# Grouped-query attention scores on four row groups of TensorE, with the maximum and the subtraction merged

## The reference, cut to what matters

```
Q = (x @ Wq.T).reshape(B, S, HKV, G, HEAD_DIM)     # HKV = 4, G = 4
K = (x @ Wk.T).reshape(B, S, HKV, HEAD_DIM)
V = (x @ Wv.T).reshape(B, S, HKV, HEAD_DIM)
scores = einsum('bskgd,bswkd->bskgw', Q, K_win) * scale
attn = softmax(scores, axis=-1)
out = einsum('bskgw,bswkd->bskgd', attn, V_win).reshape(B, S, HQ * HEAD_DIM)
return out @ Wo.T
```

## Time and profile before

| | us |
|---|---|
| median of 3 runs | 1850.55 (1847.84 to 1853.06) |
| profiled execution, device time | 1847.98 |
| its span | 1846.2 |
| PE busy | 1664.0 (90%) |
| DVE busy | 809.1 (44%) |
| ACT busy | 492.9 (27%) |
| POOL busy | 407.7 (22%) |

### The profile page before, as it was taken

How to read it: one execution, slowest core, us unless ns; L and a number is a source line. 1 busy time by engine, 2 the same in 40 slices (tenths; PEclk the granted TensorE clock), 3 DMA queues, 4 the chain that set the end, 5 groups by cost and what they waited for, 6 DMA issues and landing times.

```text
span 1846.2 us, 22813 instructions
## 1 busy us (share of the span) xinstructions
PE 1664.0 (90%) x8086; PEld 1167.7 (63%) x8086; DVE 809.1 (44%) x1724; ACT 492.9 (27%) x953; POOL 407.7 (22%) x421
## 2 busy tenths in 40 slices
PE   5876899986799999999938999999899989998999
PEld 4532355555699999999934556766764446666444
DVE  3532787776311111111157650122365556675455
ACT  1234554441112221212114322223110035544000
POOL 0363876661211111211110000000010012232000
PEclk9989899996699999999968989999789999998999
DMA  5233565554234544313130000010000010000000
GB/s 168 68 93 102 138 153 124 139 128 142 83 138 160 189 160 160 140 50 137 41 106 1 0 29 0 1 46 1 1 1 1 1 46 1 1 1 1 12 18 20
DMA packets 59046, 129.17 MB, mean 70 GB/s; under 512 B 10563, under 2 KB 39268, under 8 KB 52388
## 3 DMA queue, kind: packets, MB, share of 16 engines
q1 hardware_dynamic: 54996, 116.96, 20.3%
q0 software_dynamic: 3936, 10.75, 1.8%
HBM read 196.35 MB, written 9.97 MB: 112 GB/s over the span
## 4 chain that ended last, share of the span: by engine, by line
PE 79%; DVE 10%; POOL 3%; SPq 2%; issue 2%; DMA 2%; ACT 2%; DVEq 0%; ACTq 0%; POOLq 0%
PE psum L686 41%; PE psum L972 13%; PE psum L718 8%; PE psum L781 5%; PE psum L902 2%; PE psum L696 2%; PE psum L897 2%; DVE work L1794 1%; DVE work L1650 1%; SPq L592 1%; DVE work L1793 1%; ACT work L1072 1%; PE psum L957 1%; POOL xn L1863 1%; PE psum L981 1%
## 5 line engine op out<-in xcount | busy, mean ns | idle before, releaser
L686 PE MATMUL psum<-work 128*128 128x128 f32 (+4 forms) x3528 | 481.5, 298 | 15.9 <-DMA work<-in_xp 15.9
L686 PEld LDWEIGHTS psum<-work 128*128 128x128 f32 (+1 forms) x3528 | 451.2, 192 | 34.0 <-DMA work<-in_xp 15.9
L972 PE MATMUL psum<-w_late,xn 128*128 128x512 f32 x544 | 241.4, 602 | 0.0
L1717 DVE TENSOR_TENSOR work<-sq,psum 128x512 f32<-128x512 f32 x82 | 56.4, 688 | 388.8 <-PE psum L686 388.8
L972 PEld LDWEIGHTS psum<-w_late,xn 128*128 128x128 f32 x544 | 103.2, 192 | 128.3 <-issue 118.8
L1650 DVE TENSOR_TENSOR_SCAN work<-psum,work 128x414 f32<-128x414 f32 (+1 forms) x160 | 160.4, 1060 | 47.6 <-POOL work L1885 24.0
L1885 POOL TENSOR_TENSOR work<-work 128x408 f32<-128x408 f32 (+1 forms) x160 | 161.7, 1038 | 64.9 <-PE psum L781 47.1
L1844 POOL TENSOR_TENSOR rs<-rs,power 128x4 f32<-128x4 f32 (+3 forms) x40 | 45.1, 1130 | 577.7 <-DVE rs L1344 548.0
L1534 DVE SCALAR_TENSOR_TENSOR h<-psum,gate,h 128x256 f32<-128x256 f32 x272 | 119.3, 480 | 106.3 <-PE psum L972 103.4
L1072 ACT ACTIVATE work<-psum 68x364 f32<-68x364 f32 (+10 forms) x266 | 113.2, 466 | 144.5 <-PE psum L686 66.9
L781 PE MATMUL psum<-work,xn 128*128 128x408 f32 (+1 forms) x320 | 136.6, 560 | 14.1 <-POOL work L1885 14.0
(11 more groups left out here) (255 smaller groups left out, 1961.5 us busy)
## 6 DMA issues: line engine op xcount, KB each, us to landing
work<-in_W SPq DMA_DIRECT2D x123, 1024.0 KB
work<-c_rows SPq DMA_DIRECT2D x48, 204.0 KB, 4.1
w_attn<-in_B SPq DMA_DIRECT2D x64, 128.0 KB, 2.5
w_attn<-in_A SPq DMA_DIRECT2D x64, 128.0 KB, 2.8
work<-c_rows SPq DMA_DIRECT2D x32, 238.0 KB, 4.0
w_attn<-in_A SPq DMA_DIRECT2D x64, 64.0 KB, 2.2
w_attn<-in_B SPq DMA_DIRECT2D x64, 64.0 KB, 2.8
work<-y_rows SPq DMA_DIRECT2D x8, 512.0 KB, 7.6
```

Source lines behind the costliest of these rows:

```text
L686: mm = pe.matmul(dst, lhs(k), rhs(k), start=(k == 0), stop=(k == parts - 1))
L972: mm = pe.matmul(dst.rearrange("p (e n) -> p e n", e=2), xn[:, k, i * P:(i + 1) * P], w_last[:, 2 * q:2 * q + 2, k, :], start=(k == 0), st ...
L1717: dve.tensor_tensor(hm[:, j % 2, 4 * q:4 * q + 4, :].rearrange("p k n -> p (k n)"), sa[:, i % 2], A.at(("e3", j, q)), ALU.mult).then_inc(s ...
```

## The change

The keys are kept as they come, in `k3` (68 columns per batch), with one copy per chunk and no memset. Scores of one batch are 12 matmuls: for each piece and head g, the 32 rows of that head on row group g of the array (`tile_position=(g * HPAD, 0)`), 68 columns, into bank g of a new ring S4 of four banks, so a bank holds one head's three pieces. All four banks belong to one batch. shift3 then is one maximum and one subtraction over 91 x 816. Ring T (banks 4, 5, 6) takes projections, transposes and out3, ring O (bank 7) the values' product, and the layer norm of L3F has banks 4 and 5. ACT does exp3(b+2) in iteration b, where it did exp3(b+3). DVE's order is sum3(b+1), shift3(b+3), add_h.

```diff
-        kblk = carve(KR * KV_HEADS * SEQ).rearrange("p (b g s) -> p b g s", g=KV_HEADS, s=SEQ)
+        k3 = carve(KR * SEQ).rearrange("p (b s) -> p b s", s=SEQ)
...
+        S4 = Banks(psum, [0, 1, 2, 3], tenants)
+        T = Banks(psum, [4, 5, 6], tenants)
+        O = Banks(psum, [7], tenants)
...
-        ln_ring = {L0A: F, L3A: W8}
+        ln_ring = {L0A: F, L3A: W8, L3F: Banks(psum, [4, 5], tenants)}
...
         def plan_s3(b):
-            for i in range(PIECES):
-                A.plan(("s3", b, i), (sem("s3_shifted"), PIECES * b + i + 1))
+            for g in range(KV_HEADS):
+                S4.plan(("s3", b, g), (sem("s3_shifted"), b + 1))
             step("s3", b)
...
-                plan_h("out3", L3A, c)
+                plan_h("out3", L3A, c, T)
                 plan_ln_after(L3F, c, 2)
             if b < BATCH:
-                B.plan(("o3", b), (sem("o3_kept"), b + 1))
+                O.plan(("o3", b), (sem("o3_kept"), b + 1))
...
+                banks = [S4.wait_free(pe, ("s3", b, g)) for g in range(KV_HEADS)]
                 for i in range(PIECES):
-                    dst = A.wait_free(pe, ("s3", b, i))
-                    pe.matmul(dst[0:PROWS, 0:KV_HEADS * SEQ],
-                              q3[:, c % 2, b - CHUNK_B0[c], PIECE0[i]:PIECE0[i] + PROWS], kblk[:, at3(b)],
-                              start=True, stop=True).then_inc(sem("s3_done"), 1)
+                    for g in range(KV_HEADS):
+                        rows = slice(g * HPAD, (g + 1) * HPAD)
+                        mm = pe.matmul(banks[g][0:PROWS, i * SEQ:(i + 1) * SEQ],
+                                       q3[rows, c % 2, b - CHUNK_B0[c], PIECE0[i]:PIECE0[i] + PROWS], k3[rows, at3(b), :],
+                                       start=True, stop=True, tile_position=(g * HPAD, 0))
+                mm.then_inc(sem("s3_done"), 1)
...
-            act.wait_ge(sem("pool_setup"), 6)
...
-                src = A.at(("k3", c))
-                for g in range(KV_HEADS):
-                    rows = slice(g * HPAD, (g + 1) * HPAD)
-                    ins = act.activation(kblk[rows, at3(CHUNK_B0[c]):at3(CHUNK_B0[c]) + CHUNK_BATCHES[c], g, :],
-                                         seqs(src[rows, 0:ntok(c)]), ACT.Copy)
-                ins.then_inc(sem("k3_kept"), 1)
+                copy(k3[:, at3(CHUNK_B0[c]):at3(CHUNK_B0[c]) + CHUNK_BATCHES[c], :], seqs(T.at(("k3", c))[:, 0:ntok(c)]), "k3_kept")
...
-            for b in range(AHEAD):
+            for b in range(AHEAD - 1):
                 exp3(b)
...
-                if b + AHEAD < BATCH:
-                    exp3(b + AHEAD)
+                if b + AHEAD - 1 < BATCH:
+                    exp3(b + AHEAD - 1)
...
             def shift3(b):
-                for i in range(PIECES):
-                    dve.wait_ge(sem("s3_done"), PIECES * b + i + 1)
-                    s = A.at(("s3", b, i))[0:PROWS, 0:KV_HEADS * SEQ].rearrange("p (g s) -> p g s", g=KV_HEADS)
-                    mx = st3[0:PROWS, b % (AHEAD + 1), 0, i * KV_HEADS:(i + 1) * KV_HEADS]
-                    link(dve.tensor_reduce(mx, s, AX_X, ALU.max))
-                    dve.tensor_tensor(p3[0:PROWS, b % (AHEAD + 1), i], s,
-                                      mx.unsqueeze(2).to_broadcast([PROWS, KV_HEADS, SEQ]),
-                                      ALU.subtract).then_inc(sem("s3_shifted"), 1)
+                dve.wait_ge(sem("s3_done"), b + 1)
+                s = psum[0:PROWS, S4.bank["s3", b, 0]:S4.bank["s3", b, 0] + KV_HEADS, 0:PIECES * SEQ].rearrange(
+                    "p g (i s) -> p i g s", i=PIECES)
+                mx = st3[0:PROWS, b % (AHEAD + 1), 0, :].rearrange("p (i g) -> p i g", i=PIECES)
+                link(dve.tensor_reduce(mx, s, AX_X, ALU.max))
+                dve.tensor_tensor(p3[0:PROWS, b % (AHEAD + 1)], s,
+                                  mx.unsqueeze(3).to_broadcast([PROWS, PIECES, KV_HEADS, SEQ]),
+                                  ALU.subtract).then_inc(sem("s3_shifted"), 1)
...
-            shift3(0)
-            for b in range(1, AHEAD):
+            for b in range(AHEAD):
                 shift3(b)
-                sum3(b - 1)
+            sum3(0)
             for b in range(BATCH + 1):
+                if b + 1 < BATCH:
+                    sum3(b + 1)
                 if b + AHEAD < BATCH:
                     shift3(b + AHEAD)
-                if b + AHEAD - 1 < BATCH:
-                    sum3(b + AHEAD - 1)
                 if b and (b == BATCH or b in CHUNK_B0):
-                    add_h(L3A, "out3", CHUNKS - 1 if b == BATCH else CHUNK_B0.index(b) - 1)
+                    add_h(L3A, "out3", CHUNKS - 1 if b == BATCH else CHUNK_B0.index(b) - 1, T)
...
-            wait_all(pool, L2F)
-            pool.memset(kblk, 0.0).then_inc(sem("pool_setup"), 1)
```

More of the change, by code:

```diff
@@ L506, in plan_qkv3 @@
         def plan_qkv3(c):
-            A.plan(("k3", c), (sem("k3_kept"), c + 1))
+            T.plan(("k3", c), (sem("k3_kept"), c + 1))
             for j in range(V3[c]):
-                A.plan(("v3", c, j), (sem("v3_kept"), V30[c] + j + 1))
+                T.plan(("v3", c, j), (sem("v3_kept"), V30[c] + j + 1))
             step("kv3", c)
             for j in range(GROUP):
-                A.plan(("q3", c, j), (sem("q3_kept"), GROUP * c + j + 1))
+                T.plan(("q3", c, j), (sem("q3_kept"), GROUP * c + j + 1))
             step("q3", c)
         def plan_s3(b):
-            for i in range(PIECES):
-                A.plan(("s3", b, i), (sem("s3_shifted"), PIECES * b + i + 1))
+            for g in range(KV_HEADS):
+                S4.plan(("s3", b, g), (sem("s3_shifted"), b + 1))
             step("s3", b)
@@ L530, in build @@
                 for i in range(PIECES):
-                    A.plan(("pT3", b, i), (sem("pT3_kept"), PIECES * b + i + 1))
+                    T.plan(("pT3", b, i), (sem("pT3_kept"), PIECES * b + i + 1))
                 step("pT3", b)
@@ L988, in kv3 @@
                 wait_normed(pe, L3A, c)
-                dst = A.wait_free(pe, ("k3", c))
+                dst = T.wait_free(pe, ("k3", c))
                 product(dst[:, 0:ntok(c)], lambda k: wk3[:, k, :], lambda k: xn[:, k, chunk(c)],
@@ L992, in kv3 @@
                 for j in range(V3[c]):
-                    dst = A.wait_free(pe, ("v3", c, j))
+                    dst = T.wait_free(pe, ("v3", c, j))
                     for i in range(4 * j, min(4 * j + 4, CHUNK_BATCHES[c])):
@@ L1001, in q3_ @@
                 for j in range(GROUP):
-                    dst = A.wait_free(pe, ("q3", c, j))
+                    dst = T.wait_free(pe, ("q3", c, j))
                     product(dst[:, 0:ntok(c)], lambda k: wq3[:, k, j, :], lambda k: xn[:, k, chunk(c)],
@@ L1018, in pT3_ @@
                 for i in range(PIECES):
-                    dst = A.wait_free(pe, ("pT3", b, i))
+                    dst = T.wait_free(pe, ("pT3", b, i))
                     for g in range(KV_HEADS):
@@ L1027, in pv3 @@
                 pe.wait_ge(sem("v3_kept"), V30[c + 1])
-                dst = B.wait_free(pe, ("o3", b))
+                dst = O.wait_free(pe, ("o3", b))
                 pe.wait_ge(sem("pT3_kept"), PIECES * (b + 1))
@@ L1036, in out3 @@
                 pe.wait_ge(sem("o3_kept"), CHUNK_B0[c] + CHUNK_BATCHES[c])
-                into_h("out3", wo3, lambda k, cols: oT3[:, k, cols], c, GROUP)
+                into_h("out3", wo3, lambda k, cols: oT3[:, k, cols], c, GROUP, T)
             steps = {"ln": ln, "hT": hT, "tok": tok, "prims": prims, "guards": guards, "z": z, "dt": dt, "yacc": yacc,
@@ L1260, in keep_kv3 @@
                 if c >= 2:
[L1261 removed]
+                    act.wait_ge(sem("s3_done"), CHUNK_B0[c - 1])
                     act.wait_ge(sem("o3_done"), CHUNK_B0[c - 1])
[L1263 to L1268 removed]
+                copy(k3[:, at3(CHUNK_B0[c]):at3(CHUNK_B0[c]) + CHUNK_BATCHES[c], :], seqs(T.at(("k3", c))[:, 0:ntok(c)]), "k3_kept")
                 for j in range(V3[c]):
@@ L1272, in keep_kv3 @@
                     act.wait_ge(sem("v3_done"), V30[c] + j + 1)
-                    copy(vb3[0:SEQ, at3(b):at3(b) + n, :], A.at(("v3", c, j))[0:SEQ, 0:n * P].rearrange("p (b n) -> p b n", n=P),
+                    copy(vb3[0:SEQ, at3(b):at3(b) + n, :], T.at(("v3", c, j))[0:SEQ, 0:n * P].rearrange("p (b n) -> p b n", n=P),
                          "v3_kept")
@@ L1279, in keep_q3 @@
                     if c >= 2 and j == 0:
-                        act.wait_ge(sem("s3_done"), PIECES * CHUNK_B0[c - 1])
-                    copy(q3[:, c % 2, 0:CHUNK_BATCHES[c], j * SEQ:(j + 1) * SEQ], seqs(A.at(("q3", c, j))[:, 0:ntok(c)]),
+                        act.wait_ge(sem("s3_done"), CHUNK_B0[c - 1])
+                    copy(q3[:, c % 2, 0:CHUNK_BATCHES[c], j * SEQ:(j + 1) * SEQ], seqs(T.at(("q3", c, j))[:, 0:ntok(c)]),
                          "q3_kept")
             def exp3(b):
-                act.wait_ge(sem("s3_shifted"), PIECES * (b + 1))
+                act.wait_ge(sem("s3_shifted"), b + 1)
```

(10 more changed lines are left out.)

1 line of the change is left out of this document (removed).

## The result

| | before | after |
|---|---|---|
| median, us | 1851.8 (4 runs, 1847.84 to 1858.34) | 1881.24 (4 runs, 1873.44 to 1882.01) |
| profiled execution, us | 1847.98 | 1880.69 |
| its span, us | 1846.2 | 1878.9 |
| mean granted clock of its span | 0.935 | 0.902 |

The ratio is 1.0146, with a 95% interval of 1.0121 to 1.0172: slower, by 27 us. The forecast was 1847.4, and the time lies above the top of the range, 1870.

What follows compares the result with a forecast made beforehand. DVE, without a gap, was taken to bound the block's steady work, TensorE the rest. Terms +1.3 - 6.4 + 0.4 = -4.7, with +1.5 for the clock -3.2, gave 1844.8 profiled, median 1847.4; range 1839 to 1870.

Steps and rivals of the forecast that it cites:

- The costs of the change: Grouped-query block, per batch: merged maximum 0.99 us, subtraction 1.01, shift3 2.05 in all, row-group scores 0.77.
- scores to the signal: Per batch, from the first score load until DVE may start: 0.77 us, with four row groups side by side.
- transposes 9 to 11: Restart after a feed: batch 11's transposes come 6.9 us after those of batch 9.
- left at the start: Block's start with single-buffered scores: delay still left when the first feed begins, +1.3 us.
- Loads run in line: Rival: score loads don't overlap, scores cost 2.2 us to the signal, +28 us, 1878; chance 0.12.
- the clock in the stretches: Between feeds: TensorE's 2.55 of 3.46 us per batch exceeds both earlier loads, so granted clock 1.00 was expected.
- this rival: Clock falls between feeds: +0.9 us per step, +4.9 per stretch, 1867 with all four hit; chance 0.30.
- The clock at the start: Before the first feed TensorE idles longer, so the low level reaches into the feed: +1.5 us.
- ln_ring for L3F has two banks instead of six: ACT's copies there also wait for TensorE: Last layer norm: fewer banks were claimed to cost nothing.
- The gain of the stretches: Four stretches between feeds: three gain 1.5 us each, the one with seven batches 1.9, together -6.4.
- ring of 6.74 us for two batches: Steady work between feeds: the dependency cycle through DVE, POOL and TensorE takes 6.91 us per two batches, step 3.46.

Runs made afterwards that it cites:

- e9: Changed kernel with two 256-column fills per batch, six banks for the last norm, and more fills at the block's start: 1846.99 us, 0.9977.
- e3: Control: changed kernel with two extra matmuls per batch of only 8 columns, ahead of the transposes: 1881.59 us, 1.0166.
- e10: Changed kernel with each row-group score matmul issued twice, 48 passes per batch instead of 24: 1886.22 us, 1.0166.
- e2: Changed kernel with two extra matmuls of 256 columns per batch, ahead of the transposes, results overwritten: 1857.66 us, 1.0024.
- e4: Changed kernel with block-diagonal keys and wide full-row scores put back, in a ring of three banks, the rest kept: 1873.9 us, 1.0119.
- e1: Changed kernel with one extra matmul of 256 columns per batch, ahead of the transposes, result overwritten: 1859.14 us, 1.0036.
- e7: Kernel before with its last layer norm (L3F) on two banks, 4 and 5, nothing else: 1859.72 us, 1.0041.
- e8: Changed kernel with two extra 256-column matmuls per batch and six banks for the last layer norm: 1849.81 us, 0.9991.
- e6: Changed kernel with the last layer norm (L3F) on six banks instead of two, nothing else: 1872.91 us, 1.0122.
- e11: As e9, but in the stretches one extra matmul ahead of the transposes and one ahead of pv3, instead of two ahead of the transposes: 1840.58 us, 0.9943.
- e5: Kernel before with the order part alone, exponential one batch behind and sums first, wide scores and old banks: 1858.99 us, 1.0024.

## Why the prediction was wrong

**The costs of the change: right.** Maximum and subtraction 1.000 and 1.003 us (0.99 and 1.01), scores to the signal 0.78 (0.77), transposes 9 to 11 in 6.87 (6.9), the first transposes 12.0 us after the first scores when the clock holds (e9; forecast 12.0), 1.5 us left at the start (forecast 1.3). "Loads run in line" fell at once: 24 loads of 91 columns take 0.57 us. The Trainium skill (TensorE: Matmul & The Clock Gate, Part 3, The mechanism) has a load overlap the matmuls in flight where row groups differ, and this trace agrees: those 0.57 us lie inside the passes' 0.71.

**The step that failed is the one on the clock in the stretches**: "The new load is above both, which speaks against this rival". That rival had its mechanism, its place and its price, and it is what happened, in all four stretches; I gave it 0.30. The argument against it compared busy shares. In the kernel before 2.17 of 3.40 us busy were followed by 1.00; in the kernel after 2.51 of 3.40 were followed by 0.50. e3's 2.67 were followed by 0.50 as well, e10's 2.64 and 2.67 by 1.00: the busy share didn't tell. What was streamed mattered: in e3 and e2 the same instructions stand at the same places, with 8 and with 256 columns, and the times are 1.0166 and 1.0024; with wide scores (e4) the stretches hold 1.00. The prediction named the doubt itself, short passes on a quarter of the rows of which "no row shows how they hold the clock", and a doubt without a row should have kept its half of the chance. Its price fits: +0.9 per step, measured 4.16 - 3.37 = 0.8 over e1's mean step; +4.9 per stretch, measured (152.0 - 133.8) / 4 = 4.6 over e2, which keeps the clock. But with all four stretches hit it gave 1867, which is 16.4 us on the profiled pair, and that moved by 32.7: what lies beyond it is mostly the start (4.7) and the end (11.2 from transposes 27 on), the next two points.

**The clock at the start was mis-sized.** The term was +1.5 us; the low level reached from 1509.2 to 1533.1, not half of 3.4 us more, and cost 6.0 (35.1 after, 29.1 in e9). TensorE had 0.71 of 2.70 us of work before it fell, and I had counted on the level of before's start, where 4.36 us of scores came in one piece.

**"ln_ring for L3F has two banks instead of six: ACT's copies there also wait for TensorE", costed at nothing,** was the third miss: +0.41% on the kernel before by itself (e7), and when taken away with the fills in place (e8), 0.9967 of e2's ratio. The sentence looked at ACT; the wait is TensorE's, for add_h, 0.79 us, with the low clock behind it. Of the 8.0 us that the end loses, about 5 go with the banks (e6: 27.9) and the rest with the clock of the last batches (e8: 23.5), both by one profile each, and e9's 27.6 shows how far such a one can be off.

**The gain of the stretches: right, where the clock holds.** Forecast -6.4 us, of it -1.9, -1.5 and -1.5 for the first three. e1 keeps the clock in these and shows -1.7, -1.7 and -1.8, with a ring of 6.74 us for two batches (forecast 6.91), a step of 3.37. The fourth fell in e1, so the whole -6.4 was seen in no run. e2 and e11, which hold all four, show -3.8 and -3.4, but their two fills per batch take TensorE's time (e11 busy 10.40 of 10.40) and make the step 3.41 and 3.44.

**The sum again, with the clock held.** By the stages of e8, which keeps it in the stretches and at the end: start +7.6, stretches -3.8, transposes 27 to 31 -0.4, to the dense block -1.4, together +2.0 from the first score to the end. e9 turns the +7.6 into +1.5, but its norm ran at the low clock (+2.7), so that its sum is +0.8. Both ratios are lower than that (0.9991 is -1.7 us, 0.9977 is -4.3), and part of why is plain: the profiled execution of before, 1847.98, lies 3.8 below its median of 1851.8, and this seems to be the clock too: of the kernel before's executions next to the experiments, the four under 1848 us had a mean granted clock of 0.934 to 0.936, the six over 1859 us 0.928 to 0.930. So stages compared with that profile can make another kernel look worse by up to so much. The same holds for the kernel after: by the medians it loses 29.4 us (1881.24 - 1851.8), by its ratio 27, by the profiled pair 32.7.

**Open.** Why one fill held the clock in three stretches and not in the fourth (e1), and why doubled scores did in two (e10): no run took that apart. Why e11's ratio, a median of 11 runs against 22, is lower than its stages give: the 6.3 us ahead of its first score go with a higher granted clock there (0.87 and 0.79), and no edit lies ahead of it. What sets the clock in code that no edit touches, ahead of the block and in the norm of e5 and e9. Of e4 and after, how much the rows and how much the 68 columns of a pass count wasn't told apart.

## What to carry to other kernels

When a change makes TensorE's work shorter but not the ring that it stands in, ask first whether the clock will hold, and don't take the busy share of other rows as the answer: here 2.51 and 2.67 of 3.40 us were followed by the low clock, 2.17 by the high one. At the low clock TensorE itself can become the bound of a ring that DVE set before. If a trace has no row for the new kind of pass, a run with wide extra matmuls, where the engine would wait anyway, and a control with narrow ones show whether the clock is what is lost, and may be the repair. A ring of PSUM banks for a stage at the border of two blocks is not free to shrink (0.41% here): look for TensorE's wait there. And compare the clock of code that no edit touches before a difference of 0.3% is put down to the edit.

## What the runs showed of the hardware

- Full work doesn't bring the clock back at once: in the kernel after it stayed at 0.50 for 17 to 20 us in each stretch, in the second without a gap of TensorE from 1595.6 to 1608.2 (7.40 us of 7.40 busy from 1600.8).
- Passes on four row groups slow down with the clock like others: 24 passes in 0.71 us at 1.00, in 1.20 at 0.50.
- Matmuls that nobody reads can make a kernel faster: two of 256 columns per batch, 1.2% (1.0146 to 1.0024); the same two with 8 columns nothing (1.0166).
- The code up to the first score, nearly the same in all kernels here, ended between 1497.3 and 1512.1 us in the twelve profiled executions of the experiments, more than most differences that this study is about, with 211.6 us of low clock ahead of it in the earliest and 232.1 in the latest; stages are best compared from their own start.
